# Who issues the twelve transfers that stack q, and where the stacked tiles keep their heads

## The chip, the cores and the metric

The kernel runs on one core of one Trainium2 chip. The metric is device time in microseconds (us), from one launch to its end. Lower is better.

## What is computed

Thirty-two sequences of 112 tokens with 512 channels go through cross-attention over 375 context tokens each (16 heads of 32 channels), and then through a mixture of 8 experts, two per token. Cut to what matters here:

```
x = x + xattn(layernorm(x), ctx)
    q = w8a8_linear(x, wq, bq)            # dynamic int8 quantisation of the rows
    k = cond @ wk.T + bk;  v = cond @ wv.T + bv
    scores = q k^T / sqrt(32) + mask;  attn = softmax(scores);  o = attn v
    return w8a8_linear(o, wo, bo)
x = x + experts(layernorm(x))             # top 2 of 8, silu(gate) * up, down
```

## The kernel before

The program has four parts, one behind the other: `prepare_weights`, `attention`, `route` and `experts`. The change touches `attention` alone, which takes some two thirds of the time.

**Iterations and steps.** `attention` is software-pipelined by hand. Iteration `it` computes the scores and the softmax of sequence `it` (stage a), the projections of sequence `n = it + 1`, the layer norm and the quantisation of `nn = it + 2`, and the end of sequences `it - 1` and `it - 2`. `iterations` (L253) writes the first and last iterations out and makes a hardware loop over pairs of the middle ones. Within an iteration each engine walks over 16 steps, one per head `h`. The order of the work on each engine is what is written in its `body`; every engine runs its own list in order, and semaphores (`need`) tie the lists together.

**One step on TensorE (PE).** `turn_probs` of head `h - 2` (L563, three transposes), `scores` of head `h` (L555, one matmul), then a share of the 28 parts of the projections (L591 and L596, three matmuls each). At step 15 there is no projection; the output projection of the sequence before (L656) stands there. The step of head 0 begins with `turn_probs` of head 14 of the sequence before.

**One step on ACT.** `turn_out` of head `h - 2` (L385, copies the transposed probabilities out of PSUM), then `softmax` of head `h` (L392, exponential and row sum). Some steps have one more item: `k_hi` (L408) at steps 3, 5, 7 and 9, `q_hi` (L424) at 9, `ctx_hi` (L429) at 10, and `w_hi` (L434), a part of the expert weights' split in two, at 12.

**One step on VectorE (DVE).** Mask and row minimum of head `h` (L464), which releases the softmax on ACT and, two heads on, the next scores on PE; at step 10 `q_lo` (L502), the low part of q.

**Stacking.** A score matmul contracts over 96 rows: three groups of 32 rows that hold (q_hi, q_hi, q_lo) in `q_stack` and (k_hi, k_lo, k_hi) in `k_stack`. In `q_hi` and the others, head `h = 4g + i` lies in rows 32i to 32i + 31 of column group g, so the heads of one row group are 0, 4, 8 and 12 steps apart. DMA transfers move these from one row group to another: twelve per sequence for q, and twenty-four for k in two halves of twelve (`stack_keys`, L274), all issued by SyncE (SP). `k_stack` holds head `h` at place `h`, and `q_stack` too, so a transfer of k writes two pieces per row (`8 * half + i:8 * half + 8:4`) and a transfer of q four pieces of 448 bytes per row (`i:H:4`).

**SP's list in one iteration.** The second half of the keys (12 transfers), two loads of expert weights, the mask, two stores and a load of x; then the first half of the keys of the next sequence (12), the twelve of q (L312 to L317), the context load of `n3 = it + 3` (L321), a load of x, and four stores of the split expert weights (L327, L328).

**Who waits for q.** `scores` of head 0 waits for all twelve transfers:

```python
                if h == 0:
                    need(pe, q_stacked, 16 * QDMAS * (b + 1))
```

and ACT's `q_hi` of the next sequence waits for them before it overwrites the source (L423). The transfers themselves wait for `q_out` at `3 * n + 3`, which is DVE's `q_lo`.

Of the kernel before, what the change touches and what calls it, by code (L numbers as in the profile page):

```python
# [4 lines left out]
F32 = mybir.dt.float32  # L5
# [7 lines left out]
H = 16  # L13
# [5 lines left out]
QUARTER = 32  # L19
# [141 lines left out]
def attention(nc, W, x, ctx_t, mask, x1, h2):  # L161
# [6 lines left out]
    B, N, C = x.shape  # L168
    L = ctx_t.shape[2]
    LP = L + L % 2  # L170
    KT = C // 128
    G4 = H // 4
# [8 lines left out]
    with ExitStack() as ctx:  # L181
# [3 lines left out]
        proj, score, turn = [bank("proj0"), bank("proj1")], [bank("score0"), bank("score1")], [bank("turn0"), bank("turn1")]  # L185
# [5 lines left out]
        k_st = sb("k_stack", [96, H, LP], F32R)  # L191
        q_hi, q_lo = sb("q_hi", [128, G4, N], F32R), sb("q_lo", [128, G4, N], F32R)
# [47 lines left out]
        def need(eng, s, count):  # L240

            if not isinstance(count, int) or count > 0:
                eng.wait_ge(s, count)
# [28 lines left out]
        @block.sync  # L272
        def _(sp):
            def stack_keys(half):  # L274

                for i in range(4):
                    rows = slice(QUARTER * i, QUARTER * i + QUARTER)
                    for r, src in ((0, k_hi), (1, k_lo), (2, k_hi)):
                        sp.dma_start(k_st[QUARTER * r:QUARTER * r + QUARTER, 8 * half + i:8 * half + 8:4, :].bitcast(F32),
                                     src[rows, 2 * half:2 * half + 2, :].bitcast(F32)).then_inc(k_stacked[half], 16)  # L280

            def body(it, par, inside=False):
                has_m2, has_m, has_a, has_n, has_nn, has_n3 = stages(it, inside)
                n, m, m2, n3 = it + 1, it - 1, it - 2, it + 3
                if has_a:
                    need(sp, unit_out, UNITS * it + KT)
                    if inside or it > 0:
                        waited(sp)
                        need(sp, scored, H * it)
                    stack_keys(1)  # L290
                    need(sp, w_stored, 64 * it)
                    sp.dma_start(w_raw[:, 0:WG], W["gate_up_flat"][:, bass.ds(it * WG, WG)]).then_inc(w_in, 16)
                    sp.dma_start(w_raw[:, WG:WG + WD], W["down_flat"][:, bass.ds(it * WD, WD)]).then_inc(w_in, 16)
                if has_n:
                    need(sp, masked, H * (n - 1))
                    sp.dma_start(neg_mask[:, (par + 1) % 2, :], mask[n, :, :]).then_inc(mask_in, 16)
                if has_m2:
                    need(sp, x1_steps, 2 * m2 + 2)
                    sp.dma_start(x1[m2, :, :], x1_s[:, :]).then_inc(x1_stored, 16)
                    need(sp, ln2, 3 * m2 + 3)  # L300
                    sp.dma_start(h2[m2, :, :], h2_s[:, :]).then_inc(h2_stored, 16)
                if has_m:
                    need(sp, x1_steps, 2 * m)
                    sp.dma_start(x_res[:, :], x[m, :, :]).then_inc(x_res_ld, 16)
                if has_n:
                    q = (par + 1) % 2
                    need(sp, unit_out, UNITS * n + KT // 2)
                    if has_a:
                        waited(sp)
                        need(sp, scored, H * it + H // 2)  # L310
                    stack_keys(0)
                    need(sp, q_out, 3 * n + 3)  # L312
                    for i in range(4):
                        rows = slice(QUARTER * i, QUARTER * i + QUARTER)
                        for r, src in ((0, q_hi), (1, q_hi), (2, q_lo)):
                            sp.dma_start(q_st[QUARTER * r:QUARTER * r + QUARTER, q, i:H:4, :].bitcast(F32),
                                         src[rows, :, :].bitcast(F32)).then_inc(q_stacked, 16)  # L317
                if has_n3 and (inside or n3 > 0):
                    need(sp, c_lo_made, n3)
                    need(sp, c_hi_made, n3)  # L320
                    sp.dma_start(stage[:, :, 0:L], ctx_t[n3, :, :].rearrange("(t p) l -> p t l", p=128)).then_inc(ctx_in, 16)  # L321
                    need(sp, ln1, 8 * (n3 - 2) + 8)
                    sp.dma_start(x_in[:, (par + 3) % 2, :], x[n3, :, :]).then_inc(x_in_ld, 16)
                if has_a:
                    need(sp, w_lo_made, it + 1)
                    for src, gate_up_part, down_part in ((w_hi, "gate_up_hi", "down_hi"), (w_lo, "gate_up_lo", "down_lo")):
                        sp.dma_start(W[gate_up_part][:, bass.ds(it * WG, WG)], src[:, 0:WG].bitcast(F32)).then_inc(w_stored, 16)  # L327
                        sp.dma_start(W[down_part][:, bass.ds(it * WD, WD)], src[:, WG:WG + WD].bitcast(F32)).then_inc(w_stored, 16)  # L328

            iterations(sp, body)  # L330
            sp.wait_ge(x1_stored, 16 * B)
            sp.wait_ge(h2_stored, 16 * B)
            sp.wait_ge(w_stored, 64 * B)
# [46 lines left out]
        def _(act):  # L380
# [14 lines left out]
            def body(it, par, inside=False):  # L395
                has_m2, has_m, has_a, has_n, has_nn, _ = stages(it, inside)
                n, m, m2, nn = it + 1, it - 1, it - 2, it + 2
                for h in range(H):
                    if h < 2 and has_m:
                        turn_out(m, H - 2 + h)  # L400
                    if h >= 2 and has_a:
                        turn_out(it, h - 2)
                    if h in (3, 5, 7, 9) and has_n:
                        g = h // 2 - 1
                        need(act, unit_made, UNITS * n + g + 1)
                        if g % 2 == 0:
                            need(act, k_stacked[g // 2], 16 * KDMAS * n)
                        act.activation(k_hi[:, g, :], proj[(par + 1 + g) % 2][:, 0:LP], ACT.Identity,  # L408
                                       bias=W["bk_col"][:, g:g + 1]).then_inc(k_hi_made, 1)
                    if has_a:  # L410
                        softmax(it, par, h)
                    if h == 2 and has_m:
                        need(act, valued, H // GH * (m + 1))
                        need(act, o_made, 3 * (m - 1) + 1)
                        act.activation(out_ts[:, :, :], out_t[:, 0:G4 * N].rearrange("p (g n) -> p g n", g=G4),
                                       ACT.Copy).then_inc(out_t_out, 1)
                    if h == 4 and has_m2:
                        need(act, r_made, 2 * m2 + 1)
                        act.activation(h2_t[:, :, :], misc[:, 0:KT * N].rearrange("p (t n) -> p t n", t=KT),
                                       ACT.Copy).then_inc(r_out, 1)  # L420
                    if h == 9 and has_n:
                        need(act, q_made, 3 * n + 3)
                        need(act, q_stacked, 16 * QDMAS * n)  # L423
                        act.activation(q_hi[:, :, :], misc[:, 0:G4 * N].rearrange("p (g n) -> p g n", g=G4),  # L424
                                       ACT.Identity).then_inc(q_hi_made, 1)
                    if h == 10 and has_nn and (inside or nn > 0):
                        need(act, ctx_in, 16 * (nn + 1))
                        need(act, unit_made, UNITS * (nn - 1))
                        act.activation(c_hi[:, par % 2, :, :], stage[:, :, :], ACT.Identity).then_inc(c_hi_made, 1)  # L429

                    if h == 12 and has_a:
                        need(act, w_in, 32 * (it + 1))
                        need(act, w_stored, 64 * it)
                        act.activation(w_hi[:, :], w_raw[:, :], ACT.Identity).then_inc(w_hi_made, 1)  # L434
# [110 lines left out]

        @block.tensor
        def _(pe):
            def scores(b, par, h):
                k = b * H + h
                if h % 8 == 0:  # L550
                    need(pe, k_stacked[h // 8], 16 * KDMAS * (b + 1))
                if h == 0:
                    need(pe, q_stacked, 16 * QDMAS * (b + 1))
                need(pe, masked, k - 1)
                pe.matmul(score[h % 2][0:N, 0:LP], q_st[:, par % 2, h, :], k_st[:, h, :],  # L555
                          start=True, stop=True).then_inc(scored, 1)

            def turn_probs(b, h):
# [621 lines left out]
```

## Time and profile before

| | |
|---|---|
| time, median of 3 runs | 1607.95 us (1605.15 to 1608.63) |
| the profiled execution's own time | 1609.71 us |
| its span, first to last instruction | 1608.0 us |
| granted TensorE clock, mean over the span | 0.965 |
| busy: PE, PE weight loads, DVE, ACT, POOL | 93%, 82%, 56%, 55%, 41% |
| q1, the queue of SP's transfers: packets, MB, share of 16 engines | 203952, 247.24, 54.3% |
| score matmul of head 0, first sequence and last | at 59.18 and at 1063.39 us |
| from one sequence's head 0 to the next, from the sixth on | 32.0 to 32.4 us |

How to read it: the span is that of the profiled execution, 1.7 us shorter than its own time; both lie within 2 us of the median. Busy times are the hardware profiler's. DMA-issuing instructions are not counted as busy, so SP has no busy figure, though its list of transfers takes most of an iteration.

### The profile page before, as it was taken

To read this page: it belongs to the slowest core of one execution; us is meant where nothing else is said; L and a number is where in the kernel's file an instruction comes from. 1 tells how busy PE (TensorE), PEld (TensorE's weight loads), DVE (VectorE), ACT (ScalarE), POOL (GpSimd) and SP (SyncE) were. 2 spreads that over 40 slices of the span, in tenths; PEclk is the share of its full clock that TensorE was granted. 3 is DMA by queue.
4 is the path that set the end of the run, shared out by engine and by line. 5 is a ranking of instruction groups with operands and counts; after the bars stand their busy time and mean duration, and the time that the engine had idled before them with its cause. 6 is when DMAs were issued, how large, how long until landed. Compare 5 with 4: busy or idle time off the path is not lost. (4 is left out here: it accounts for less than half of the span.)

```text
span 1608.0 us, 40123 instructions
## 1 busy us (share of the span) xinstructions
PE 1494.6 (93%) x11594; PEld 1317.6 (82%) x11595; DVE 897.5 (56%) x2365; ACT 884.0 (55%) x2097; POOL 660.6 (41%) x671
## 2 busy tenths in 40 slices
PE   2899999999999999999999999984399999999896
PEld 2788888888888888888888888873299999999895
DVE  6557666766676667666766676654632222222221
ACT  2467667677777776777677767761033333333232
POOL 4233334333443234323432343323555555656453
PEclk9999999999999999999999999985599999999998
DMA  5567777677767776777677767654537776666643
GB/s 173 145 170 196 209 200 197 179 228 205 194 178 226 202 196 179 225 205 196 178 225 201 200 179 222 185 142 141 160 68 186 182 175 134 148 154 125 160 77 48
DMA packets 220124, 281.09 MB, mean 175 GB/s; under 512 B 83568, under 2 KB 164976, under 8 KB 220080
## 3 DMA queue, kind: packets, MB, share of 16 engines
q1 hardware_dynamic: 203952, 247.24, 54.3%
q0 software_dynamic: 16128, 33.30, 11.6%
q8 instruction: 23, 0.38, 0.1%
q14 instruction: 21, 0.17, 0.0%
HBM read 118.31 MB, written 66.17 MB: 115 GB/s over the span
## 5 line engine op out<-in xcount | busy, mean ns | idle before, releaser
L464 DVE CUSTOM_DVE_ANT_0 probs<-score,neg_mask 112x375 f32<-112x375 f32 x512 | 279.7, 546 | 254.8 <-PE score L555 251.5
L392 ACT ACTIVATE probs<-probs,neg_max 112x375 f32<-112x375 f32 x512 | 312.3, 610 | 197.2 <-DVE neg_max L464 191.7
L563 PE MATMUL turn<-ident,probs 112*125 112x112 f32 x1536 | 264.8, 282 | 2.8 <-ACT probs L392 2.5
L385 ACT ACTIVATE probs_t<-turn 125x336 f32<-125x336 f32 x512 | 226.0, 441 | 71.6 <-PE turn L563 70.6
L563 PEld LDWEIGHTS turn<-ident,probs 112*125 112x125 f32 x1536 | 227.2, 190 | 36.4 <-issue 14.4
L555 PE MATMUL score<-k_stack,q_stack 96*112 96x376 f32 x512 | 209.4, 409 | 8.5 <-DMA q_stack<-q_lo 6.2
L591 PE MATMUL proj<-ctx_hi,wk_hi 128*128 128x376 f32 x512 | 176.0, 344 | 1.9 <-PEq L29 1.1
L591 PE MATMUL proj<-ctx_lo,wk_hi 128*128 128x376 f32 x512 | 172.0, 336 | 0.0
L591 PE MATMUL proj<-ctx_hi,wk_lo 128*128 128x376 f32 x512 | 171.7, 335 | 0.0
L1032 DVE TENSOR_TENSOR a_lo<-a_ps,a_hi 128x384 fp32r<-128x384 f32 x63 | 35.1, 557 | 243.7 <-ACT a_hi L1007 243.7
L596 PE MATMUL proj<-wv_hi,ctx_hi 128*125 128x512 f32 x384 | 151.8, 395 | 0.0
L596 PE MATMUL proj<-wv_hi,ctx_lo 128*125 128x512 f32 x384 | 151.7, 395 | 0.0
L596 PE MATMUL proj<-wv_lo,ctx_hi 128*125 128x512 f32 x384 | 151.0, 393 | 0.0
L354 POOL TENSOR_SCALAR neg_mask<-neg_mask 112x375 f32<-112x375 f32 x32 | 16.8, 525 | 305.2 <-DMA neg_mask<-mask 305.2
L370 POOL TENSOR_TENSOR ctx_lo<-ctx_stage,ctx_hi 128x1504 fp32r<-128x1504 f32 x31 | 106.6, 3437 | 57.9 <-ACT ctx_hi L429 57.9
L990 POOL DMA_INDIRECT out<-y_rows,scatter_idx x63 | 101.9, 1618 | 57.3 <-POOL scatter_idx L986 50.7
L375 POOL TENSOR_TENSOR w_raw<-w_raw,w_hi 128x1056 fp32r<-128x1056 f32 x32 | 78.9, 2467 | 92.9 <-ACT w_hi L434 92.9
L591 PEld LDWEIGHTS proj<-ctx_hi,wk_hi 128*128 128x128 f32 x512 | 97.4, 190 | 8.7 <-issue 1.5
L1020 ACT ACTIVATE y_rows<-y_ps,row_share 128x512 f32<-128x512 f32 x63 | 43.5, 691 | 106.7 <-PE y_ps L1102 73.3
L555 PEld LDWEIGHTS score<-k_stack,q_stack 96*112 96x112 f32 x512 | 92.4, 181 | 9.9 <-issue 7.5
L591 PEld LDWEIGHTS proj<-ctx_lo,wk_hi 128*128 128x128 f32 x512 | 97.6, 191 | 0.0
L591 PEld LDWEIGHTS proj<-ctx_hi,wk_lo 128*128 128x128 f32 x512 | 96.9, 189 | 0.0
(198 smaller groups left out, 3393.9 us busy)
## 6 DMA issues: line engine op xcount, KB each, us to landing
k_stack<-k_hi SPq DMA_DIRECT2D x512, 94.0 KB, 2.2
k_stack<-k_lo SPq DMA_DIRECT2D x256, 94.0 KB, 2.2
ctx_stage<-ctx_t SPq DMA_DIRECT2D x32, 750.0 KB, 5.0
q_stack<-q_hi SPq DMA_DIRECT2D x256, 56.0 KB, 2.0
w_raw<-gate_up_t SPq DMA_DIRECT2D x32, 352.0 KB, 3.1
gate_up_dram_hi<-w_hi SPq DMA_DIRECT2D x32, 352.0 KB, 4.8
gate_up_dram_lo<-w_raw SPq DMA_DIRECT2D x32, 352.0 KB, 5.2
gate_up_hi<-gate_up_dram_hi SPq DMA_DIRECT2D x16, 704.0 KB, 4.9
```

What stands on the lines that cost most here:

```text
L370: pool.tensor_tensor(c_lo[:, par % 2, :, :], stage[:, :, :], c_hi[:, par % 2, :, :].bitcast(F32), ALU.subtract).then_inc(c_lo_made, 1)
L375: pool.tensor_tensor(w_lo[:, :], w_raw[:, :], w_hi[:, :].bitcast(F32), ALU.subtract).then_inc(w_lo_made, 1)
L385: act.activation(probs_t[:, h % RING_T, :, :], turn[h % 2][0:LC, 0:LT * N].rearrange("p (l n) -> p l n", l=LT), ACT.Copy).then_inc(turned_ ...
L392: act.activation(probs[:, h % DS, :], probs[:, h % DS, :], ACT.Exp, bias=neg_max[:, par % 2, h:h + 1], scale=-1.0, accum_out=total[:, par ...
L464: dve.tensor_tensor_reduce(probs[:, h % DS, :], score[h % 2][0:N, 0:L], neg_mask[:, p, :], 1.0, BIG, ALU.add, ALU.min, neg_max[:, p, h:h + ...
L555: pe.matmul(score[h % 2][0:N, 0:LP], q_st[:, par % 2, h, :], k_st[:, h, :], start=True, stop=True).then_inc(scored, 1)
L563: mm = pe.transpose(turn[h % 2][0:LC, l * N:(l + 1) * N], probs[:, h % DS, l * LC:(l + 1) * LC], W["ident"][0:N, 0:N])
L591: mm = pe.matmul(bank[:, 0:LP], W[w][:, t, 128 * u:128 * u + 128], c[:, q, t, :], start=(t == 0 and w == "wk_hi" and c is c_hi), stop=(t = ...
L596: mm = pe.matmul(bank[0:LC, :], c[:, q, t, l * LC:(l + 1) * LC], W[w][:, t, :], start=(t == 0 and w == "wv_hi" and c is c_hi), stop=(t == ...
L990: pool.indirect_dma_start(out, bass.IndirectOffsetOnAxis(ap=si[par][:, 0:1], axis=0), y[:, par, :], None, compute_op=ALU.add).then_inc(sca ...
L1020: act.activation(y[:, other, :], y_ps[other][:, 0:C], ACT.Copy, scale=share[:, other:other + 1]).then_inc(y_made, 1)
L1032: dve.tensor_tensor(a_lo[:, :], a_ps[:, 0:FP], a_hi[:, :].bitcast(F32), ALU.subtract).then_inc(a_lo_made, 1)
```

## The change

The twelve q transfers go from SP's list to ACT's. ACT issues four of them behind the softmax of head 12, four behind that of head 13 and four behind that of head 14 (q_hi into row group 0, q_hi into row group 1, q_lo into row group 2). At step 12 they stand ahead of `w_hi`. The stacked tiles keep the heads in another order: head `h` lies at place `h % 4 * 4 + h // 4`, so that the heads of one source row group lie beside each other. Each transfer of k and of q then writes one contiguous piece per row.

```diff
@@ stack_keys (SP)
-                        sp.dma_start(k_st[QUARTER * r:QUARTER * r + QUARTER, 8 * half + i:8 * half + 8:4, :].bitcast(F32),
+                        sp.dma_start(k_st[QUARTER * r:QUARTER * r + QUARTER, G4 * i + 2 * half:G4 * i + 2 * half + 2, :].bitcast(F32),
                                      src[rows, 2 * half:2 * half + 2, :].bitcast(F32)).then_inc(k_stacked[half], 16)
@@ body (SP)
                 if has_n:
-                    q = (par + 1) % 2
                     need(sp, unit_out, UNITS * n + KT // 2)
...
                     stack_keys(0)
-                    need(sp, q_out, 3 * n + 3)
-                    for i in range(4):
-                        rows = slice(QUARTER * i, QUARTER * i + QUARTER)
-                        for r, src in ((0, q_hi), (1, q_hi), (2, q_lo)):
-                            sp.dma_start(q_st[QUARTER * r:QUARTER * r + QUARTER, q, i:H:4, :].bitcast(F32),
-                                         src[rows, :, :].bitcast(F32)).then_inc(q_stacked, 16)
@@ body (ACT), behind the softmax of head h and ahead of w_hi
+                    if h in (12, 13, 14) and has_n:
+                        need(act, q_out, 3 * n + 3)
+                        r, src = ((0, q_hi), (1, q_hi), (2, q_lo))[h - 12]
+                        for i in range(4):
+                            act.dma_start(q_st[QUARTER * r:QUARTER * r + QUARTER, (par + 1) % 2, G4 * i:G4 * i + G4, :].bitcast(F32),
+                                          src[QUARTER * i:QUARTER * i + QUARTER, :, :].bitcast(F32)).then_inc(q_stacked, 16)
@@ scores (PE)
+            def stacked_at(h):
+
+                return h % 4 * G4 + h // 4
+
-                pe.matmul(score[h % 2][0:N, 0:LP], q_st[:, par % 2, h, :], k_st[:, h, :],
+                pe.matmul(score[h % 2][0:N, 0:LP], q_st[:, par % 2, stacked_at(h), :], k_st[:, stacked_at(h), :],
                           start=True, stop=True).then_inc(scored, 1)
```

Lines behind L306 stand seven lower in the changed kernel up to the new block: what was L392 is L385 there, and what was L385 is L378.

ACT's list before, from the softmax of head 12 to that of head 15 of one iteration (`probs,total` is the softmax, `probs_t` is `turn_out`):

```order
L392 ACTIVATE probs,total<-probs,neg_max 112x375 [waits masked]
L434 ACTIVATE w_hi<-w_raw 128x1056 [waits w_stored,w_in]
L385 ACTIVATE probs_t<-turn 125x336 [waits valued,turned]
L392 ACTIVATE probs,total<-probs,neg_max 112x375 [waits masked]
L385 ACTIVATE probs_t<-turn 125x336 [waits valued,turned]
L392 ACTIVATE probs,total<-probs,neg_max 112x375 [waits masked]
L385 ACTIVATE probs_t<-turn 125x336 [waits valued,turned]
L392 ACTIVATE probs,total<-probs,neg_max 112x375 [waits masked]
```

and the same place now:

```order
L385 ACTIVATE probs,total<-probs,neg_max 112x375 [waits masked]
L428 DMA q_stack<-q_hi 32x448 [waits q_out]
L428 DMA q_stack<-q_hi 32x448 x3
L433 ACTIVATE w_hi<-w_raw 128x1056 [waits w_stored,w_in]
L378 ACTIVATE probs_t<-turn 125x336 [waits valued,turned]
L385 ACTIVATE probs,total<-probs,neg_max 112x375 [waits masked]
L428 DMA q_stack<-q_hi 32x448 [waits q_out]
L428 DMA q_stack<-q_hi 32x448 x3
L378 ACTIVATE probs_t<-turn 125x336 [waits valued,turned]
L385 ACTIVATE probs,total<-probs,neg_max 112x375 [waits masked]
L428 DMA q_stack<-q_lo 32x448 [waits q_out]
L428 DMA q_stack<-q_lo 32x448 x3
```

The last four transfers stand behind the softmax of head 14, one `turn_out` and one softmax ahead of the end of the iteration.

SP's list before, around the q transfers of one iteration (the rows ahead are the end of the first half of the keys):

```order
L279 DMA k_stack<-k_hi 32x2x376
L316 DMA q_stack<-q_hi 32x4x112 [waits q_out]
L316 DMA q_stack<-q_hi 32x4x112
L316 DMA q_stack<-q_lo 32x4x112
...
L321 DMA ctx_stage<-ctx_t 128x4x375 [waits c_hi_made,c_lo_made]
```

and now:

```order
L279 DMA k_stack<-k_hi 32x752
L314 DMA ctx_stage<-ctx_t 128x4x375 [waits c_hi_made,c_lo_made]
L316 DMA x_in<-x 112x512 [waits ln1]
L320 DMA gate_up_dram_hi<-w_hi 128x704 [waits w_lo_made]
```

A key transfer is now 32 rows of 752 numbers in place of 32 x 2 x 376, and a q transfer 32 rows of 448 in place of 32 x 4 x 112; the context load follows the keys directly.

## Rows read from the trace of the kernel before

**Rows 1.** The page: busy time of PE, the granted clock in 40 slices, the packets.

```profile
PE 1494.6 (93%) x11594; PEld 1317.6 (82%) x11595; DVE 897.5 (56%) x2365; ACT 884.0 (55%) x2097; POOL 660.6 (41%) x671
...
PEclk9999999999999999999999999985599999999998
...
DMA packets 220124, 281.09 MB, mean 175 GB/s; under 512 B 83568, under 2 KB 164976, under 8 KB 220080
```

**Rows 2.** Windows: stretch, length, busy of PE, PEld, DVE, ACT, POOL, PEclk, DMA share, GB/s.

```profile
400.00:1000.00 600.00, 599.72 (x5193) 516.77 (x5191) 416.99 (x1176) 427.15 (x1059) 220.72 (x187) 1.00 0.72 199
```

**Rows 3.** Timeline, PE, score of head 0, first six sequences: start, duration, [idle before <-releaser].

```profile
59.18 0.63 PE L555 MATMUL score<-k_stack,q_stack 96*112 96x376 f32 x1 [3.60 <-DMA q_stack<-q_lo]
...
90.88 0.40 PE L555 MATMUL score<-k_stack,q_stack 96*112 96x376 f32 x1 [1.33 <-issue]
...
123.72 0.40 PE L555 MATMUL score<-k_stack,q_stack 96*112 96x376 f32 x1 [0.41 <-issue]
...
156.52 0.42 PE L555 MATMUL score<-k_stack,q_stack 96*112 96x376 f32 x1 [0.58 <-DMA q_stack<-q_lo]
...
190.18 0.42 PE L555 MATMUL score<-k_stack,q_stack 96*112 96x376 f32 x1 [1.32 <-DMA q_stack<-q_lo]
...
224.76 0.42 PE L555 MATMUL score<-k_stack,q_stack 96*112 96x376 f32 x1 [0.67 <-DMA q_stack<-q_lo]
```

**Rows 4.** Timeline, PE, a steady iteration: transposes of heads 13 and 14, score 0.

```profile
642.49 0.48 PE L563 MATMUL turn<-ident,probs 112*125 112x112 f32 x3
...
643.84 0.48 PE L563 MATMUL turn<-ident,probs 112*125 112x112 f32 x3
644.09 0.40 PE L555 MATMUL score<-k_stack,q_stack 96*112 96x376 f32 x1
```

**Rows 5.** Timeline, ACT, the same stretch: softmax of heads 12, 13, 14 and between.

```profile
638.74 0.61 ACT L392 ACTIVATE probs<-probs,neg_max 112x375 f32<-112x375 f32 x1 [1.14 <-DVE neg_max L464]
...
639.35 1.07 ACT L434 ACTIVATE w_hi<-w_raw 128x1056 fp32r<-128x1056 f32 x1
640.33 0.43 ACT L385 ACTIVATE probs_t<-turn 125x336 f32<-125x336 f32 x1
641.05 0.61 ACT L392 ACTIVATE probs<-probs,neg_max 112x375 f32<-112x375 f32 x1 [0.29 <-DVE neg_max L464]
...
642.41 0.61 ACT L392 ACTIVATE probs<-probs,neg_max 112x375 f32<-112x375 f32 x1 [0.32 <-DVE neg_max L464]
```

**Rows 6.** Timeline, SP: the last q transfer of three iterations, and what follows.

```profile
57.04 0.60 SPq L316 DMA_DIRECT2D q_stack<-q_lo  x1
...
88.79 0.60 SPq L316 DMA_DIRECT2D q_stack<-q_lo  x1
...
640.79 0.60 SPq L316 DMA_DIRECT2D q_stack<-q_lo  x1
641.72 0.43 SPq L321 DMA_DIRECT2D ctx_stage<-ctx_t  x1
```

**Rows 7.** Timeline, SP: transfers with one contiguous piece per row.

```profile
136.47 0.43 SPq L296 DMA_DIRECT2D neg_mask<-mask  x1
136.94 0.42 SPq L299 DMA_DIRECT2D out<-y  x1
...
642.42 0.33 SPq L323 DMA_DIRECT2D x_in<-x  x1
```

**Rows 8.** The page, DMA issues: KB each, median us from issue to landing.

```profile
q_stack<-q_hi SPq DMA_DIRECT2D x256, 56.0 KB, 2.0
```

**Rows 9.** Windows behind two waits of PE, columns as in rows 2.

```profile
59.18:66.00 6.82, 6.82 (x26) 6.81 (x27) 1.67 (x6) 2.62 (x8) 0.00 (x0) 0.56 0.97 272
66.00:72.80 6.80, 6.80 (x49) 6.61 (x48) 3.99 (x12) 5.65 (x16) 0.52 (x1) 1.00 0.52 145
...
186.00:192.80 6.80, 5.48 (x33) 4.61 (x32) 5.03 (x16) 3.91 (x13) 2.07 (x2) 1.00 0.61 157
```

**Rows 10.** Timelines of the first sequence: DVE's q_lo, PE's last projection.

```profile
49.19 0.62 DVE L502 TENSOR_TENSOR q_lo<-misc,q_hi 128x448 fp32r<-128x448 f32 x1 [0.22 <-ACT q_hi L424]
...
55.18 0.40 PE L596 MATMUL proj<-wv_hi,ctx_lo 128*125 128x512 f32 x1
```

## The prediction

> **What bounds the kernel now.** I read the page first. PE is busy for 93% of the span and its clock stands at the top in nearly every slice [rows 1]; the two dips are at the end of attention and beyond, which the change doesn't touch. Then the windows: from 400 to 1000 us PE is busy for 599.72 of 600 us at clock 1.00, while DVE and ACT have some 30% free [rows 2]. So in steady state the time of attention is PE's own work, and nothing that relieves SP, ACT or the DMA engines can shorten it. What can change it is a wait that PE does not have now. Third, the timeline of PE at the score of head 0, the one place that waits for q: it waited in the first six sequences only, 3.60 us once and then 1.33, 0.41, 0.58, 1.32 and 0.67 [rows 3]. There SP runs late with the last q transfer (57.04, 88.79). From the seventh on the wait is gone. In the iteration that I take as the pattern, SP's last q transfer starts at 640.79 and the score at 644.09 [rows 4, 6]: 3.3 us between them, for a transfer that needs 2.0 to 2.1.
>
> That margin is where the change acts. It takes the transfers from an engine that is ready for them at about 633 us and gives them to one that reaches the last four only behind its softmax of head 14, which starts at 642.41 [rows 5], 1.68 us ahead of the score that needs them.
>
> **The price of an issue on ACT.** No ACT issue stands in this trace. The nearest rows are SP's. A q transfer in four pieces per row takes 0.60 us of SP [rows 6]; transfers of one piece per row take 0.43 and start 0.47 apart where the program is written out, and one in the loop took 0.33 [rows 7]. The changed q transfer has one piece per row and a fixed address, so I take 0.43, and 0.48 from start to start. The ends are 0 (ACT need not pay what SP pays) and 0.64 (it pays as for the old shape). The Trainium skill (SBUF — State Buffer, The DMA setup-cost knee) puts the setup at about 50 ns for the sequencer and a few hundred ns for descriptor generation. With the first of these alone the sum would come out near the first rival.
>
> **Landing.** The page has 2.0 us from issue to landing [rows 8]; PE's score at 90.88 followed the issue at 88.79 by 2.09 us, 1.49 behind the issue's end [rows 3, 6]. With an issue of 0.43 that gives 1.9 us from its start; the bounds are 1.5 and 2.1.
>
> **The steady iteration, step by step** (times as in rows 4 and 5; ACT's sequencer is taken to go on to the transfers as soon as it has handed the softmax to the datapath):
> - Head 12: softmax at 638.74 as before; four issues until about 640.7; w_hi from 640.7 in place of 639.35, 0.98 us; turn_out at 641.7 in place of 640.33, 0.4 us; softmax of head 13 at 642.1 in place of 641.05.
> - Head 13: its softmax was released at 641.05, so the issues run beside w_hi, from 641.1 to 643.0; turn_out at 643.0; softmax of head 14 at 643.4 in place of 642.41.
> - Head 14: handed over at about 643.05, issues start at 643.1, 643.6, 644.1 and 644.54. The last lands 1.92 later, at 646.46.
> - Score of head 0 at 646.46 in place of 644.09: **a wait of 2.4 us**. The transposes of head 14 (643.84) come some 0.3 late for the softmax of head 14; that lies inside the 2.4. The softmax of head 15 is ready at about 646.3, a microsecond ahead of its use.
>
> Queued behind the issues are turn_out and softmax (inside the wait, as shown) and w_hi, 1.35 us later; behind it come POOL's low part and SP's four stores, which have SP's freed time as cover: SP now goes on at about 638 instead of 641.4. The next keys are issued from there and needed eight heads on. Were SP late again, the score of head 8 would wait.
>
> There are 31 such places (sequences 1 to 31): 31 x 2.4 = **+74 us**. None of it is made up later, since PE has no idle time to give back [rows 2].
>
> **What comes back.** The five waits of the early sequences are replaced, not added to: 1.33 + 0.41 + 0.58 + 1.32 + 0.67 = -4.3. For sequence 0, q_lo is done at 49.8 and PE at 55.6 [rows 10]. ACT issues from 49.8 beside SP's keys: twelve at 0.48, the last starts at 55.1 and lands at 57.0; the score starts there instead of 59.18, -2.2. The clock was at half (0.56 mean, 26 matmuls) for 6.8 us behind the 3.60 us wait, where the next 6.8 us held 49 [rows 9]; with a wait of 1.4 it should stay up, as behind the 1.32 us wait at 190.18 [rows 3, 9]: 6.8 / 2 = -3.4. Together -9.9.
>
> **What costs nothing.** Twelve fewer issues and twenty-four shorter ones on SP, 12 x 0.64 + 24 x 0.17 = 12 us per iteration: SP holds nothing up after the sixth sequence. The 49152 q pieces of 448 bytes (384 transfers x 32 x 4), most of the 83568 packets under 512 B [rows 1], become 12288 of 1792: the DMA engines are busy 0.72 [rows 2], and nobody but that score waits for them. The new order of heads in the tiles changes addresses of the score matmuls alone, still one contiguous row each: 0, since the weight load and the matmul have their old sizes.
>
> Sum: +74 - 10 = +64 on the profiled execution's 1609.7 us, or 1674; the median of the runs is 1.8 lower, so I say **1672 us**.
>
> **Rivals.**
> 1. *An issue costs ACT next to nothing* (0 to 0.1 us). Nothing on ACT shifts, the last transfer starts at about 642.6 and lands at 644.1 to 644.7, so the wait is 0 to 0.6: 31 x 0.3 = +9, less 10: about 1607, from 1598 to 1617. For it: the pace of rows 6 and 7 may be SP's alone. Against it: rows 7 have 0.33 even at the simplest shape. Its lower end is the **faster** case: landing within 1.5 us of the start, no new wait at all, and the early waits gone, 1598. It decides below 0.05 us per issue.
> 2. *Each wait drops the clock.* Behind 3.60 us of idle PE ran 6.8 us at the lower level, 1.2 GHz; behind 1.32 it did not [rows 3, 9]. 2.4 lies between. If every wait is followed by such a stretch, 31 x 3.4 = +105 on top: 1777; for one in three, 1707. The Trainium skill (TensorE: Matmul & The Clock Gate, What's actually happening) calls half rate the state of an idle array and full rate that of a busy one. By that rule an array that idles for 2.4 us in 34 stays up; the rows agree up to 1.32 us, and none of them tests a length between that and 3.60.
> 3. *ACT's issues wait until its datapath has finished.* Then batch 1 runs from 639.45 to 641.4, softmax 13 ends at 643.5, batch 2 at 645.5, softmax 14 at 646.7, the last issue starts at 648.1 and lands at 650.0: a wait of 5.9, 31 x 5.9 - 10 = +173, 1781, and more with the clock. The Trainium skill (PSUM — Partial Sum Buffer, Engine vs sequencer instructions) says that the sequencer waits only until earlier instructions are dispatched; by that rule this falls. No row of this trace shows it.
> 4. *The old price per issue* (0.64): last start at 646.0, landing at 648.1, a wait of 4.0: 31 x 4.0 - 4 = +120, 1728.
> 5. *The change does not do what it says*: if the pieces had not merged, case 4 is what comes. The built program shows 32x448 and 32x752, so I give this nothing of its own.
>
> **How the numbers follow.** My case (a wait of 1.5 to 3.2 us, clock mostly up; 1643 to 1700) 0.50; clock drops at most places (1700 to 1780) 0.20; datapath wait or old price (1720 and above) 0.15; cheap issue 0.15, of which faster 0.08. A measurement of this kernel tells 0.2%, 3.2 us, from no change. Faster 0.08, same 0.06, slower 0.86. The range leaves out the faster end (0.08) and what lies above 1780 (some 0.1): **1612 to 1780**.
>
> **What the profile would show.** Right: PE score of head 0 waits for a q transfer in every sequence, about 2.4 us; ACT issues of 0.43 us, the last 1.9 us ahead of the score; w_hi some 1.4 us later behind head 12; the distance from one head 0 to the next near 34.6 us instead of 32.2; clock 1.00 around them; the packets under 512 B down to about 34000. Wrong: issues below 0.1 us (rival 1), half-clock stretches once per sequence (rival 2), ACT issues that start at the end of the softmax, not near its start (rival 3), a wait at head 8 for keys, or a PE that catches up behind the wait.

## The result: 15% slower, where 4% were forecast

| | before | changed |
|---|---|---|
| time, median | 1608.29 us (1605.15 to 1610.07, 4 runs) | 1854.38 us (1846.48 to 1863.85, 4 runs) |
| ratio, 95% interval | | 1.1535 (1.1477 to 1.1594) |
| span of the profiled execution | 1608.0 us | 1850.6 us |
| mean granted clock | 0.965 | 0.921 |
| score of head 0, first and last sequence | 59.18, 1063.39 | 62.45, 1305.63 |
| mean distance of two heads 0, 7th to last sequence | 32.26 us | 40.31 us |

The forecast was 1672 us, with a range up to 1780. The direction was right, the size was not: +246 us, where +64 were forecast. The last line of the table holds nearly all of it: 25 x 8.05 = 201 us of the 242.6 between the two spans; the six sequences ahead give 38, the start of attention 3, and everything behind it is as long as before (545.0 against 544.6).

The page of the changed kernel, in answer to [rows 1] and [rows 8]; the last four lines are its queues and DMA issues (KB each, median us to landing):

```profile
PE 1581.2 (85%) x11594; PEld 1384.9 (75%) x11595; DVE 958.6 (52%) x2365; ACT 888.2 (48%) x2097; POOL 660.1 (36%) x671
...
PEclk9899999998999999899999989999757999999998
...
DMA packets 158684, 281.09 MB, mean 152 GB/s; under 512 B 34416, under 2 KB 78960, under 8 KB 158640
...
q10 hardware_dynamic: 18432, 22.04, 5.5%
...
k_stack<-k_hi SPq DMA_DIRECT2D x512, 94.0 KB, 2.2
...
q_stack<-q_hi ACTq DMA_DIRECT2D x256, 56.0 KB, 3.6
```

PE does the same 11594 matmuls but is busy for 87 us more: the clock was lower, the work is the same. The pieces did merge (under 512 B from 83568 to 34416), and a transfer of q_hi now takes 3.6 us to land in place of 2.0 (medians; q_lo 3.0 in place of 2.0).

PE at the score of head 0, four steady sequences, in answer to [rows 3] (start, duration, [idle before <-releaser]):

```profile
621.41 0.56 PE L558 MATMUL score<-k_stack,q_stack 96*112 96x376 f32 x1 [3.73 <-DMA q_stack<-q_lo]
...
661.34 0.65 PE L558 MATMUL score<-k_stack,q_stack 96*112 96x376 f32 x1 [4.53 <-DMA q_stack<-q_lo]
...
701.00 0.65 PE L558 MATMUL score<-k_stack,q_stack 96*112 96x376 f32 x1 [3.87 <-DMA q_stack<-q_lo]
...
741.59 0.65 PE L558 MATMUL score<-k_stack,q_stack 96*112 96x376 f32 x1 [4.12 <-DMA q_stack<-q_lo]
```

Every sequence from the second on waits 3.6 to 4.6 us there, 4.15 in the mean from the eighth on. The score matmul itself takes 0.65 us, not 0.40: it runs at half rate. The windows behind the wait, columns as in [rows 2], in answer to [rows 9]:

```profile
701.00:707.80 6.80, 6.80 (x32) 6.47 (x36) 2.93 (x8) 2.85 (x8) 1.28 (x1) 0.57 0.67 175
707.80:714.60 6.80, 6.80 (x89) 6.51 (x82) 2.84 (x10) 5.13 (x15) 1.28 (x3) 1.00 0.70 212
```

The same picture as behind the one long wait of the kernel before, once per sequence. And ACT's timeline in the stretch that the prediction walked through, in answer to [rows 5] (ACTq is what its sequencer issues):

```profile
690.01 0.61 ACT L385 ACTIVATE probs<-probs,neg_max 112x375 f32<-112x375 f32 x1 [1.14 <-DVE neg_max L463]
690.02 0.54 ACTq L428 DMA_DIRECT2D q_stack<-q_hi  x1
...
690.60 1.89 ACTq L428 DMA_DIRECT2D q_stack<-q_hi  x3
692.68 1.09 ACT L433 ACTIVATE w_hi<-w_raw 128x1056 fp32r<-128x1056 f32 x1 [1.96 <-issue]
...
694.00 0.60 ACT L385 ACTIVATE probs<-probs,neg_max 112x375 f32<-112x375 f32 x1
...
695.60 0.52 ACTq L428 DMA_DIRECT2D q_stack<-q_lo  x1
695.80 0.60 ACT L385 ACTIVATE probs<-probs,neg_max 112x375 f32<-112x375 f32 x1
696.15 0.61 ACTq L428 DMA_DIRECT2D q_stack<-q_lo  x1
...
696.79 1.30 ACTq L428 DMA_DIRECT2D q_stack<-q_lo  x2
```

The issues start 0.01 us behind the start of the softmax, beside it: the sequencer does run ahead of the datapath. But they take 0.61 us each (median) and are 0.64 apart from start to start, and w_hi comes 2.67 us behind the softmax's start, where it came 0.61 behind it.

SP in the same stretch, in answer to [rows 6]:

```profile
689.44 0.41 SPq L314 DMA_DIRECT2D ctx_stage<-ctx_t  x1
...
696.38 0.38 SPq L320 DMA_DIRECT2D gate_up_dram_hi<-w_hi  x1
696.85 0.56 SPq L321 DMA_DIRECT2D down_dram_hi<-w_hi  x1
697.50 0.60 SPq L320 DMA_DIRECT2D gate_up_dram_lo<-w_raw  x1
698.19 0.65 SPq L321 DMA_DIRECT2D down_dram_lo<-w_raw  x1
699.10 0.54 SPq L279 DMA_DIRECT2D k_stack<-k_hi  x1
```

The last q transfer is issued at 697.4, in the middle of four stores of 1056 KB together, and lands at 701.0. Before, these stores came 2.3 us behind the last q transfer of the iteration (at 640.79, [rows 6]):

```profile
643.08 0.38 SPq L327 DMA_DIRECT2D gate_up_dram_hi<-w_hi  x1
```

### The profile page after: what moved, and what is told of

The parts are those of the page before. It is cut to its first block and busy times, and to the rows that moved or that the text cites. A ratio compares the mean times of both kernels' runs of the same rounds, so it can differ in the third digit from the quotient of the medians.

```text
span 1850.6 us, 40097 instructions
## 1 busy us (share of the span) xinstructions
PE 1581.2 (85%) x11594; PEld 1384.9 (75%) x11595; DVE 958.6 (52%) x2365; ACT 888.2 (48%) x2097; POOL 660.1 (36%) x671
## 2 busy tenths in 40 slices
DMA packets 158684, 281.09 MB, mean 152 GB/s; under 512 B 34416, under 2 KB 78960, under 8 KB 158640
## 5 line engine op out<-in xcount | busy, mean ns | idle before, releaser
L385 ACT ACTIVATE probs<-probs,neg_max 112x375 f32<-112x375 f32 x512 | 310.9, 607 | 269.2 <-DVE neg_max L463 267.2
L558 PE MATMUL score<-k_stack,q_stack 96*112 96x376 f32 x512 | 227.4, 444 | 135.0 <-DMA q_stack<-q_lo 115.2
L566 PE MATMUL turn<-ident,probs 112*125 112x112 f32 x1536 | 284.8, 298 | 32.9 <-ACT probs L385 32.6
L378 ACT ACTIVATE probs_t<-turn 125x336 f32<-125x336 f32 x512 | 228.1, 446 | 173.9 <-PE turn L566 140.9
L566 PEld LDWEIGHTS turn<-ident,probs 112*125 112x125 f32 x1536 | 243.9, 205 | 79.8 <-ACT probs L385 52.6
L594 PE MATMUL proj<-ctx_hi,wk_hi 128*128 128x376 f32 x512 | 196.5, 384 | 1.9 <-PEq L29 1.1
L594 PE MATMUL proj<-ctx_lo,wk_hi 128*128 128x376 f32 x512 | 190.1, 371 | 0.0
L594 PE MATMUL proj<-ctx_hi,wk_lo 128*128 128x376 f32 x512 | 189.1, 369 | 0.0
L350 POOL TENSOR_TENSOR q_tok<-q_tok,bq_row 112x512 f32<-112x512 f32 x32 | 41.5, 1296 | 256.7 <-DVE q_tok L497 256.7
L337 POOL TENSOR_TENSOR y<-y,x_res 112x512 f32<-112x512 f32 x32 | 41.0, 1282 | 226.4 <-DVE y L469 226.4
L594 PEld LDWEIGHTS proj<-ctx_hi,wk_hi 128*128 128x128 f32 x512 | 113.4, 222 | 9.8 <-issue 1.3
L594 PEld LDWEIGHTS proj<-ctx_lo,wk_hi 128*128 128x128 f32 x512 | 113.3, 221 | 0.0
```

The source lines that it names most:

```text
L378: act.activation(probs_t[:, h % RING_T, :, :], turn[h % 2][0:LC, 0:LT * N].rearrange("p (l n) -> p l n", l=LT), ACT.Copy).then_inc(turned_ ...
L385: act.activation(probs[:, h % DS, :], probs[:, h % DS, :], ACT.Exp, bias=neg_max[:, par % 2, h:h + 1], scale=-1.0, accum_out=total[:, par ...
L558: pe.matmul(score[h % 2][0:N, 0:LP], q_st[:, par % 2, stacked_at(h), :], k_st[:, stacked_at(h), :], start=True, stop=True).then_inc(scored, 1)
L566: mm = pe.transpose(turn[h % 2][0:LC, l * N:(l + 1) * N], probs[:, h % DS, l * LC:(l + 1) * LC], W["ident"][0:N, 0:N])
L594: mm = pe.matmul(bank[:, 0:LP], W[w][:, t, 128 * u:128 * u + 128], c[:, q, t, :], start=(t == 0 and w == "wk_hi" and c is c_hi), stop=(t = ...
```

## The experiments

All are compared with the kernel before at 1607 to 1608 us. "Distance" is the mean distance of two heads 0 from the seventh sequence on, read from the profiled execution. Where no number of runs stands, the time is that of one execution. The four executions of the changed kernel lie 17 us apart, which is 0.7 us per sequence if all of it falls into the 25 distances: differences in distance of that size between two single executions are not certain.

### The two halves of the change apart

`layout_only`: the changed kernel's tiles, SP issues.

```diff
@@ body (SP), behind stack_keys(0)
+                    need(sp, q_out, 3 * n + 3)
+                    for i in range(4):
+                        rows = slice(QUARTER * i, QUARTER * i + QUARTER)
+                        for r, src in ((0, q_hi), (1, q_hi), (2, q_lo)):
+                            sp.dma_start(q_st[QUARTER * r:QUARTER * r + QUARTER, (par + 1) % 2, G4 * i:G4 * i + G4, :].bitcast(F32),
+                                         src[rows, :, :].bitcast(F32)).then_inc(q_stacked, 16)
@@ body (ACT)
-                    if h in (12, 13, 14) and has_n:
...
```

> SP issues the q transfers as before, the tiles hold the heads in the new order. Theory (the late issue on ACT and the clock drop behind it make all of the +246 us): no difference from before, 1603 to 1611 us, no wait of PE at score 0 from the seventh sequence on, clock 1.00; a transfer of one piece per row still takes SP 0.59 us, as in the changed kernel. Rival (the new places of the heads cost something, or the larger pieces save SP time): more than 5 us off before in either direction.

Measured: 1604.86 us (10 runs), ratio 0.9978 (0.996 to 0.9997), distance 32.27. The issues of k stay at 0.59 us (0.60 before), so the 24 x 0.17 us that the prediction let SP save do not come; nothing waits for SP there. The theory holds: one contiguous piece per row has no part in the loss. The prediction priced it at nothing; here it gains 3.5 us (0.5 to 6.4 by the interval).

`act_old_places`: ACT issues, heads at their old places.

```diff
-                        sp.dma_start(k_st[QUARTER * r:QUARTER * r + QUARTER, G4 * i + 2 * half:G4 * i + 2 * half + 2, :].bitcast(F32),
+                        sp.dma_start(k_st[QUARTER * r:QUARTER * r + QUARTER, 8 * half + i:8 * half + 8:4, :].bitcast(F32),
...
-                            act.dma_start(q_st[QUARTER * r:QUARTER * r + QUARTER, (par + 1) % 2, G4 * i:G4 * i + G4, :].bitcast(F32),
+                            act.dma_start(q_st[QUARTER * r:QUARTER * r + QUARTER, (par + 1) % 2, i:H:4, :].bitcast(F32),
...
-                return h % 4 * G4 + h // 4
+                return h
```

> ACT issues the q transfers as in the changed kernel, the tiles hold the heads as before (four pieces per row for q, two for k). Theory: the place of issue is all, 1840 to 1870 us, issues of about 0.62 us, a wait of 4 to 4.7 us at score 0, one half-rate stretch per sequence. Rival (the shape matters for issue or landing): landing longer by half a microsecond or more per sequence, 1870 us or above.

Measured: 1871.64 us, distance 40.92, a mean wait of 4.50 us in the last 25 sequences (4.15 with the new places). The whole loss is there without the new places. The 17 us on top lie just inside the rival's range, though its condition (landing longer by half a microsecond) is not met: with four pieces per row an issue is 0.62 us and the median landing of q_lo 3.2 against 3.0. Whether small pieces cost something when they travel beside other transfers is not shown: 0.6 us per sequence is within what executions of one kernel differ by. In SP's two kernels both shapes land in 2.0 us.

### The clock, by filling the wait

`filled_wait`: the twenty added matmuls write what nobody reads.

```diff
+                need(pe, masked, k - 1)
+                if h == 0 and fill_from is not None:
...
+                    for _ in range(20):
+                        pe.matmul(score[0][0:N, 0:LP], W["wk_hi"][:, 0, 0:N], c_hi[:, (par + 1) % 2, 0, :],
+                                  start=True, stop=True)
                 if h == 0:
                     need(pe, q_stacked, 16 * QDMAS * (b + 1))
```

> The changed kernel with twenty matmuls of no use (128x112 weights, 376 columns, their result is overwritten) on PE just ahead of its wait for q in 31 sequences; they need 20 x 0.17 = 3.4 us at full rate, less than the wait of 3.6 to 4.6. Theory (the half-rate stretch behind the wait costs 3 us per sequence): the clock stays at 1.00 through attention, the distance between two heads 0 falls from 40.4 to about 37.4 us, the time to about 1760 us. Rival (PE has time to spare behind the wait, or the clock drops for another reason): 1850 us or above.

Measured: 1778.32 us, distance 37.84. PE's timeline and the windows behind it:

```profile
659.94 3.62 PE L560 MATMUL score<-ctx_hi,wk_hi 128*112 128x376 f32 x20
664.51 0.43 PE L564 MATMUL score<-k_stack,q_stack 96*112 96x376 f32 x1 [0.95 <-DMA q_stack<-q_lo]
```

```profile
664.50:671.30 6.80, 6.79 (x82) 6.36 (x83) 3.61 (x12) 4.11 (x11) 2.03 (x3) 1.00 0.68 156
```

With 620 matmuls more, the kernel is 76 us faster. The score comes when q lands, as before, and behind it 82 matmuls fit into 6.8 us where 32 did. The half-rate stretch costs 40.31 - 37.84 = **2.5 us per sequence**. I had expected 3, and 1760 us. In the changed kernel the stretches are 6.1 us long in the mean (154 us in 25, by the clock records), half of which is 3.1. But 0.9 us of each lies inside the wait, where a slow PE costs nothing; half of the other 5.3 us is 2.6, close to the 2.5 that the distance shows.

### The landing, by holding the stores

`stores_held`:

```diff
                     need(sp, w_lo_made, it + 1)
+                    if has_n:
+                        waited(sp)
+                        need(sp, q_stacked, 16 * QDMAS * (n + 1))
```

> The changed kernel, with SP's four stores of expert weights held back until all q transfers have landed. Theory (the last q transfers land 3.6 us after their start, not 2.0, because these stores run beside them): the last landing falls to 2.0 to 2.4 us, PE's wait from 4.1 to about 2.8 us; if the clock then stays up, 1700 us or so, if it drops as before, about 1810 us. Rival (four transfers into one row group, or ACT's queue itself, make them slow): landing and wait as in the changed kernel, 1850 us or above.

Measured: 1789.80 us, distance 38.09. Median landing of q_lo is back at 2.0 us, and PE's wait is 2.5:

```profile
q_stack<-q_lo ACTq DMA_DIRECT2D x128, 56.0 KB, 2.0
```

```profile
630.54 0.42 PE L561 MATMUL score<-k_stack,q_stack 96*112 96x376 f32 x1 [2.48 <-DMA q_stack<-q_lo]
...
668.49 0.42 PE L561 MATMUL score<-k_stack,q_stack 96*112 96x376 f32 x1 [2.53 <-DMA q_stack<-q_lo]
```

```profile
630.50:637.30 6.80, 6.76 (x72) 6.37 (x72) 3.12 (x9) 2.89 (x8) 1.41 (x2) 0.75 0.73 233
```

So the long landing of the last four comes from SP's stores beside them; ACT's queue and the common destination rows are cleared. The four transfers behind head 12, issued 0.6 us and more behind the 750 KB context load, still take 4.8 us (median), and they are early enough; that the load is what slows them was not tested apart. And the clock still falls behind each of the waits of 2.5 us from the seventh sequence on, though for 4.0 us on average (99 us in 25 stretches) in place of 6.1. That is the very length of wait that I had forecast, and had taken to be harmless. The length alone does not decide it: in the third sequence of the same run PE waited for longer and stayed at full rate.

```profile
134.79 0.40 PE L561 MATMUL score<-k_stack,q_stack 96*112 96x376 f32 x1 [2.77 <-issue]
```

```profile
134.80:141.60 6.80, 6.80 (x82) 6.39 (x83) 3.69 (x12) 4.25 (x12) 2.03 (x3) 1.00 0.76 245
```

`stores_held_filled`: the same, with twelve added matmuls ahead of the wait; what they write is overwritten.

```diff
+                    for _ in range(12):
+                        pe.matmul(score[0][0:N, 0:LP], W["wk_hi"][:, 0, 0:N], c_hi[:, (par + 1) % 2, 0, :],
+                                  start=True, stop=True)
```

> The changed kernel with both: SP's four stores held until q has landed (PE's wait 2.5 us) and twelve matmuls of no use (2.0 us) ahead of that wait. Theory (the three terms add: lateness of the last issue, landing beside the stores, half-rate stretch): the clock stays up, 4.64 / 2 = 2.3 us less per sequence than with the held stores alone, about 35.7 us from one head 0 to the next, 1720 us. Rival (the clock drop costs less than its length halved, because PE would wait elsewhere): 1760 us or above.

Measured: 1729.89 us, distance 36.14, clock 1.00 from the seventh sequence to the last, waits of 0.2 us behind the added matmuls. Expected were 35.7 and 1720: the three terms add to within 0.4 us per sequence. The clock's part is 38.09 - 36.14 = 1.95, not 2.3: the expectation put the shorter stretches at 4.64 us, and the clock records have 4.0, half of which is 2.0. This gives the ledger of a sequence:

| | us | from |
|---|---|---|
| the last issue is late | 3.88 | 36.14 (`stores_held_filled`) - 32.26 (before) |
| landing beside the stores | 1.70 | 37.84 (`filled_wait`) - 36.14 |
| half-rate stretch | 2.47 | 40.31 (changed) - 37.84 |
| sum | 8.05 | 40.31 - 32.26 |

The rows are differences of neighbours, so that they add up is no test of them. Taken in the other order, landing costs 40.31 - 38.09 = 2.22 and the clock 1.95: a longer wait also makes the stretch longer.

### The place on ACT

`two_steps_earlier`:

```diff
-                    if h in (12, 13, 14) and has_n:
+                    if h in (10, 11, 12) and has_n:
...
-                        r, src = ((0, q_hi), (1, q_hi), (2, q_lo))[h - 12]
+                        r, src = ((0, q_hi), (1, q_hi), (2, q_lo))[h - 10]
```

> The changed kernel with the three groups of four issues behind the softmax of heads 10, 11 and 12 in place of 12, 13 and 14, some 4 us earlier against the score of head 0. Theory (the lateness of the last transfer is what counts): the wait at score 0 falls to 0 to 1.5 us, the clock stays up, what is left is ACT's own lag of about 1 us per sequence: 1610 to 1680 us. Rival (7.7 us of issue time on ACT is what counts, wherever it stands): 1750 us or above.

Measured: 1668.70 us, distance 34.28, no wait for q above 0.3 us and no half-rate stretch in steady state. All twelve issues still stand on ACT, so of the 8.05 us the place makes 6.0. The last four now start before SP's stores and travel beside the context load; they land in 4.6 us (median), and in time. What is left is two waits of PE for the softmax:

```profile
639.53 0.58 PE L566 MATMUL turn<-ident,probs 112*125 112x112 f32 x3 [0.68 <-ACT probs L385]
...
643.22 0.57 PE L566 MATMUL turn<-ident,probs 112*125 112x112 f32 x3 [1.04 <-ACT probs L385]
```

The second goes back to VectorE: the mask of head 15 stands behind one instruction at four times its length, beside one on POOL:

```profile
638.76 2.67 DVE L446 TENSOR_SCALAR x_in<-x_in,x_inv 112x512 f32<-112x512 f32 x1
```

```profile
638.72 2.42 POOL L368 TENSOR_TENSOR w_raw<-w_raw,w_hi 128x1056 fp32r<-128x1056 f32 x1 [4.66 <-ACT w_hi L433]
```

`two_steps_w_hi_first`: w_hi also goes ahead of the last group of issues.

```diff
+                    if h == 12 and has_a:
+                        need(act, w_in, 32 * (it + 1))
+                        need(act, w_stored, 64 * it)
+                        act.activation(w_hi[:, :], w_raw[:, :], ACT.Identity).then_inc(w_hi_made, 1)
-                    if h in (12, 13, 14) and has_n:
+                    if h in (10, 11, 12) and has_n:
```

> The groups of four behind the softmax of heads 10, 11 and 12, and w_hi ahead of the last group in place of behind it. Theory (of the 2.0 us per sequence that were left with the groups two steps earlier, 1.0 is VectorE's x_in multiply, which took 2.67 us in place of 0.66 because it ran beside POOL's subtraction behind a late w_hi): that multiply back at 0.5 to 0.7 us, no wait of PE for the softmax of head 15, about 1 us less per sequence, 1635 to 1645 us. Rival (the wait comes from ACT's own lag): 1660 us or above.

Measured: 1634.20 us, distance 33.00, and no wait of PE for the softmax. The multiply is back at 0.65 us (median), since POOL's subtraction now starts 2.1 us ahead of it:

```profile
619.15 2.46 POOL L368 TENSOR_TENSOR w_raw<-w_raw,w_hi 128x1056 fp32r<-128x1056 f32 x1 [2.61 <-ACT w_hi L427]
```

```profile
621.24 0.65 DVE L446 TENSOR_SCALAR x_in<-x_in,x_inv 112x512 f32<-112x512 f32 x1
```

The two instructions still overlap by 0.37 us here, and the multiply is 0.65 where others of its size take 0.49. The Trainium skill (SBUF — State Buffer, Who interferes with whom) says that VectorE and GpSimd share a pair of ports, that a tensor_scalar can need it and that the later of the two is blocked for the whole of the other's instruction. In both kernels the multiply ends 0.28 to 0.29 us behind POOL's end, at 641.43 and at 621.89: the trace agrees that it is blocked until then, though what it has left to do afterwards is less than its own 0.49.

The distance fell by 1.28 us, a little more than the expected 1. What is left over the kernel before is 0.74 us per sequence, and of that 0.48 is PE's wait for q at head 0, which comes back in 23 of the last 25 sequences: the last four transfers still need 4.5 us (median) beside the context load. In the changed kernel itself the multiply was held up too (median 2.67 us), but there the mask behind it was due inside the wait for q, so that it cost nothing.

### The price of an issue

`issue_probe`: `layout_only` with ten added transfers on SP and on ACT, ahead of attention.

```diff
+            for k in range(2):
+                for j, (rows, dst, shape) in enumerate(((32, 32, "flat"), (128, 0, "flat"), (32, 32, "split"), (32, 32, "dram"), (128, 0, "dram"))):
+                    d = base + 5 * k + j
+                    if shape == "dram":
+                        eng.dma_start(probe[dst:dst + rows, d, :], wq[0:rows, 0:448]).then_inc(probed, 16)
...
+                    else:
+                        eng.dma_start(probe[dst:dst + rows, d, :], raw["q"][0:rows, 0, 0:448]).then_inc(probed, 16)
```

> The kernel with SP issuing and the new order, plus ten transfers on SP and the same ten on ACT before attention, into tiles nobody reads: SBUF to SBUF with 32 rows of 448 numbers, 128 rows of 448, 32 rows of 4 x 112, and DRAM to SBUF with 32 rows and 128 rows of 448. Theory A (SBUF to SBUF costs more to issue than DRAM to SBUF, whatever the rows): 0.6 us for the first three, 0.33 to 0.45 for the last two. Theory B (32 rows cost more than 128): 0.6 us for the three of 32 rows, 0.33 to 0.45 for the two of 128. Theory C (the queue's fill sets it): neither. ACT's price equals SP's within 0.05 us in each.

Measured, from the timelines of both engines:

| | SP | ACT |
|---|---|---|
| SBUF to SBUF, 32 rows of 448 | 0.57 | 0.58, 0.61 |
| SBUF to SBUF, 128 rows of 448 | 0.58, 0.59 | 0.61, 0.61 |
| SBUF to SBUF, 32 rows of 4 x 112 | 0.65, 0.70 | 0.66, 0.71 |
| DRAM to SBUF, 32 rows of 448 | 0.59, 0.59 | 0.61, 0.76 |
| DRAM to SBUF, 128 rows of 448 | 0.42, 0.43 | 0.43, 0.44 |

(A first issue of 2.34 us on SP, behind a row of other loads, is left out.) Neither A nor B as they were put: only the loads of 128 rows from DRAM are cheap, and every other shape with one piece per row costs 0.57 to 0.61, but for one of 0.76 on ACT. What makes the difference stays open. What is settled is the mistake: I priced a transfer of 32 rows within SBUF by rows of 112-row transfers to and from DRAM [rows 7]. ACT's price is SP's, within 0.04 us, but for that one.

### A version that beats both

`split_start`: SP issues as before, in the new order of heads; for sequence 0 alone, ACT takes six.

```diff
+                    if h == 12 and not inside and it == -1:
+                        need(act, q_out, 3 * n + 3)
+                        for i in range(2):
...
@@ body (SP)
+                    for i in range(2 if not inside and it == -1 else 0, 4):
...
```

> SP issues the q transfers with the heads in the new order; for sequence 0 alone ACT, which is idle then, issues six of the twelve and SP the other six at the same time. Theory: the last one starts about 3.8 us earlier, PE's first wait of 3.3 to 3.6 us goes and with it the half-rate stretch behind it (3.4 us): 6 to 7 us less than the kernel with the new order alone, 1596 to 1600 us against 1607 of before. Rival (the transfers of the two queues hold each other up, or SP's later lateness eats the gain): no difference from the new order alone, 1603 to 1607 us.

Measured: 1601.53 us (7 runs), ratio 0.997 (0.9959 to 0.9982). The first score is at 54.88 instead of 59.18 with no wait and no half-rate stretch, and the seventh head 0 at 248.0, 5.5 us ahead of `layout_only`. Of these the span keeps 2.9. At the last head 0 it is still 5.1; the rest goes behind it, which I have not followed. The time misses the expected 1596 to 1600 by 1.5 us and lies just below the rival's 1603 to 1607. Against `layout_only` the times decide nothing, since the two ratios' intervals overlap (0.9959 to 0.9982, 0.996 to 0.9997); that the split start gains is seen in the traces of one execution each.

`split_start_mask`: the same, and the mask load on ACT:

```diff
@@ body (ACT), behind the softmax
+                    if h == 1 and has_n:
+                        need(act, masked, H * (n - 1))
+                        act.dma_start(neg_mask[:, (par + 1) % 2, :], mask[n, :, :]).then_inc(mask_in, 16)
@@ body (SP)
-                    need(sp, masked, H * (n - 1))
-                    sp.dma_start(neg_mask[:, (par + 1) % 2, :], mask[n, :, :]).then_inc(mask_in, 16)
```

> The kernel with the split first sequence, and the mask load (one DRAM load of 112 rows per sequence) issued by ACT behind the softmax of head 1 in place of SP. Theory (one issue of 0.43 us where ACT has a microsecond to spare costs nothing, and SP's lateness in sequences 1 to 5 shrinks by half a microsecond per iteration): 1 to 4 us below the split kernel, 1597 to 1600 us. Rival (ACT has nothing to spare there either): 31 x 0.3 us or more on top, 1610 us or above.

Measured: 1601.31 us (9 runs), ratio 0.9957 (0.9941 to 0.9973). The one wait of 2.3 us for POOL's q_tok is gone and the distance is 32.32 against 32.29; the two versions can't be told apart, and the expected 1597 to 1600 us are missed. Both are faster than the kernel before, by 0.3 and 0.4%, and than the changed one.

## Why the prediction was wrong, step by step

**Right.** PE bounds, nothing that relieves SP pays, and the margin between ACT's softmax of head 14 and the score of head 0 is where it goes. The kind of wait, its place and that it comes in all sequences were right; so were the run-ahead of ACT's sequencer (rival 3 falls: 0.01 us), the merged pieces (34416 packets under 512 B, where about 34000 were forecast), and that PE gives nothing back.

**Wrong in three sizes.** From the softmax of head 12 to the score of head 0 it was 5.35 us before; the prediction made it 7.7, and it is 701.00 - 690.01 = 10.99. In this iteration the difference between forecast and trace splits into three steps:

| step, as predicted | predicted | measured | per sequence |
|---|---|---|---|
| issues "0.48 from start to start" | last start 5.80 behind softmax 12 | 7.42 | +1.6 |
| "that gives 1.9 us from its start" | 1.92, bounds 1.5 to 2.1 | 3.57 | +1.65 |
| clock at the top behind a wait of 2.4 (rival 2 had 0.20) | 0 | 2.47 | +2.5 |

Together 5.75 on the 2.4 that were forecast: 8.1, and 8.05 is measured. That it fits to 0.1 is in part luck: over 25 iterations the last q transfer starts 7.42 us behind the softmax too, but the score follows it by 3.86 in the mean, not 3.57. The first error was a choice: 0.64 stood in the text as the upper bound. Rival 4, which took it, has a wait of 4.0, near the ledger's 3.88, and 1728 us; `stores_held_filled`, the kernel with nothing but that lateness left, measured 1729.89. The second error was in the bounds themselves. The prediction said that SP would now go on at 638, named the four stores and filed them under freed time. It did not ask what they would meet: the change moves the last q transfers into the stretch of the stores. The third was a rule put in the place of a missing row. The rows tested waits of 1.32 and 3.60 us; the wait that came, 4.15 in the mean, is longer than both, and a wait of 2.5 is enough in steady state. The page of the Trainium skill that was cited (TensorE: Matmul & The Clock Gate, What's actually happening) was read as speaking for a clock that stays up; the trace of `stores_held` differs, with a fall behind each of the 25 waits of 2.5 us in steady state, though not behind the one of 2.77 in the third sequence.

**The errors pulled one way.** The three were treated as alternatives with a chance each, but a dear issue makes the wait longer, and a long wait makes the drop sure. Rivals 2 and 4 together give 1728 + 105 = 1833. The range should have held their sum.

**The start** was wrong in sign: -5.6 was forecast, and the first score is 3.3 us later. The twelve issues on ACT ran from 49.7 to 57.4, no shorter than SP's, and the last four took 5.4 us and more to land beside SP's context load and keys. With half of them on each engine (`split_start`) the first score did come early, at 54.88.

## What to carry to other kernels

When transfers move to another queue, write down three things for the last of them: when its issuer reaches it, what else is on the DMA engines then, and when its reader comes; moving the issue by two steps was worth 6 of 8 us here. Price an issue by a row with the same rows and the same memories at both ends. Where a wait may lower TensorE's clock, ask what the wait and the clock cost together, don't list them side by side, and measure the clock's part by filling the wait with matmuls of no use.

## What the runs showed that was not expected

- An issue on ACT holds its sequencer for 0.61 us, not the datapath. What stands behind it waits all the same: 12 x 0.64 = 7.7 us per sequence, of which 3.9 reached the score of head 0.
- A q transfer of 56 KB landed in 2.0 us on SP's list; the last of the four on ACT took 3.6 beside 1056 KB of stores and 2.0 when these were held; the four issued just behind a 750 KB load took 4.8 (median), a load that no run took away.
- In steady state a wait of 2.5 us in 38 lowered the clock from 2.4 to 1.2 GHz each of 25 times, for 4.0 us on average, and waits of 3.6 to 4.6 us did for 6.1. Waits of 2.27 us (`split_start`, once, at 102.7) and 2.77 us (`stores_held`, once, at 134.8) did not.
- VectorE's multiply of 0.66 us took 2.67 when POOL's subtraction had started 0.04 us earlier.
